# Latent attention on one NeuronCore: a third bank for the transposed scores, and the values products gathered into four runs a pair of heads

## What is computed

```
def _L1_attn_ref(x, latent_w, latent_b, Wd_w, Wd_b, out_w, out_b):
    ...
    Wdkv = x @ latent_w + latent_b
    q = jnp.einsum('btc,hcl->bhtl', x, Wd_w) + Wd_b[None, :, None, :]
    scores = jnp.einsum('bhtl,bsl->bhts', q, Wdkv) / jnp.asarray(np.sqrt(d_head), dtype=x.dtype)
    causal = jnp.tril(jnp.ones((t, t), dtype=bool))
    scores = jnp.where(causal[None, None, :, :], scores, -jnp.inf)
    attn = jax.nn.softmax(scores, axis=-1)
    y = jnp.einsum('bhts,bsl->bhtl', attn, Wdkv)
    z = jnp.transpose(y, (0, 2, 1, 3)).reshape(b, t, h * Wdkv.shape[-1])
    return z @ out_w + out_b
```

## Time and profile before

| | before |
|---|---|
| median of 3 runs | 3188.33 us |
| lowest and highest | 3187.82 and 3189.63 us |
| profiled execution | 3197.16 us |
| its span, first to last instruction | 3195.4 us |
| TensorE busy, mean granted clock | 2832.2 us (89%), 0.919 |
| VectorE busy | 2087.3 us (65%) |
| ScalarE busy | 1199.9 us (38%) |
| GpSimd busy | 836.7 us (26%) |

### The profile page before, as it was taken

One profiled execution on the slowest core, in us unless ns is written; L12 is line 12 of the kernel. 1 busy time (PEld: TensorE's weight loads), 2 busy tenths in 40 slices (PEclk: granted clock), 3 DMA queues, 4 the chain that ended last, 5 costly groups with the idle time before them and its releaser, 6 DMA issues. The chain is left out here.

```text
span 3195.4 us, 55424 instructions
## 1 busy us (share of the span) xinstructions
PE 2832.2 (89%) x15400; PEld 1924.1 (60%) x15400; DVE 2087.3 (65%) x5242; ACT 1199.9 (38%) x2164; POOL 836.7 (26%) x1220
## 2 busy tenths in 40 slices
PE   5999999958787888689999998869989989999986
PEld 4777777735555555467777776445465465465453
DVE  6777777747676777577777776355556556555533
ACT  2111111127565657521111111335545545545532
POOL 1222332225555555423222332001101101111100
PEclk8999999958888788899999998879999999999988
DMA  3000000000000000110000000000000000000000
GB/s 130 0 0 0 0 0 0 1 0 2 3 2 3 2 2 2 61 44 0 0 0 0 0 0 1 0 1 1 1 2 1 1 1 1 1 1 1 1 1 27
DMA packets 12996, 23.60 MB, mean 7 GB/s; under 512 B 2306, under 2 KB 7682, under 8 KB 12804
## 3 DMA queue, kind: packets, MB, share of 16 engines
q1 hardware_dynamic: 12804, 21.22, 2.0%
HBM read 18.52 MB, written 2.10 MB: 6 GB/s over the span
## 5 line engine op out<-in xcount | busy, mean ns | idle before, releaser
L555 DVE SCALAR_TENSOR_TENSOR moe_acc<-moe_ps,moe_comb,moe_acc 128x512 f32<-128x512 f32 x896 | 661.1, 744 | 174.5 <-PE moe_ps L304 167.9
L2017 DVE CUSTOM_DVE_ANT_0 attn_masked<-attn_psm,attn_causal 128x1024 f32<-128x1024 f32 (+7 forms) x512 | 367.6, 755 | 210.4 <-PE attn_psm L1742 199.3
L1921 ACT ACTIVATE attn_probs<-attn_pse 128x512 f32<-128x512 f32 (+1 forms) x640 | 319.9, 553 | 301.6 <-PE attn_pse L1756 301.0
L304 PE MATMUL moe_ps<-moe_Wg,moe_xh 128*128 128x512 f32 x1024 | 329.4, 403 | 25.0 <-DVE moe_Wu L501 25.0
L335 PE MATMUL moe_ps<-moe_Wd,moe_ih 128*128 128x512 f32 x1024 | 337.8, 411 | 0.0
L304 PE MATMUL moe_ps<-moe_Wu,moe_xh 128*128 128x512 f32 x1024 | 337.1, 411 | 0.0
L1772 PE MATMUL attn_psy<-attn_probs,attn_V 128*64 128x512 f32 (+3 forms) x1536 | 325.5, 524 | 0.3 <-POOL attn_probs L1677 0.3
L454 POOL TENSOR_SCALAR moe_part<-consts,moe_pick,moe_prob 128x8 f32<-128x8 f32 x256 | 98.1, 398 | 752.1 <-ACT moe_prob L389 752.1
L1677 POOL TENSOR_SCALAR_AFFINE_SELECT attn_probs<-attn_probs 128x256 f32<-128x256 f32 (+1 forms) x192 | 95.1, 495 | 757.7 <-ACT attn_probs L1921 757.7
L1021 POOL TENSOR_TENSOR attn_R<-attn_R 128x1024 f32<-128x1024 f32 (+1 forms) x128 | 215.5, 1690 | 201.6 <-DVE attn_R L1365 201.4
L1756 PE MATMUL attn_pse<-attn_qS,attn_kS 110*128 110x512 f32 (+3 forms) x768 | 233.2, 394 | 21.4 <-ACT attn_probs L1921 15.2
(11 more groups left out here) (208 smaller groups left out, 4871.2 us busy)
## 6 DMA issues: line engine op xcount, KB each, us to landing
moe_stageg<-in_w_gate SPq DMA_DIRECT2D x8, 512.0 KB, 7.2
moe_stageu<-in_w_up SPq DMA_DIRECT2D x8, 512.0 KB, 8.3
moe_stageg<-in_w_down SPq DMA_DIRECT2D x8, 512.0 KB, 3.7
out<-X SPq DMA_DIRECT2D x1, 2048.0 KB, 8.9
attn_qS<-attn_mh SPq DMA_DIRECT2D x64, 4.0 KB
attn_qS<-attn_ml SPq DMA_DIRECT2D x64, 4.0 KB
attn_wd<-in_wd SPq DMA_DIRECT2D x1, 864.0 KB, 5.7
attn_w<-in_wqkv SPq DMA_DIRECT2D x1, 768.0 KB, 5.1
```

What stands on the lines that cost most here:

```text
L304: last = pe.matmul(expert_bank[j % 4][:, :], a[q][:, :], w[b][:, cols], start=k == 0, stop=k == 2)
L555: dve.scalar_tensor_tensor(acc[:, q, r, :], expert_bank[j % 4][:, :], comb[:, q, r, e:e + 1], acc[:, q, r, :], ALU.mult, ALU.add).then_inc ...
L1921: act.activation(probs[:, u % 2, c, HALF - n:HALF], e_bank[c][:, HALF - n:HALF], ACT.Exp, scale=SCORE_SCALE).then_inc(p_ready, 1)
L2017: dve.tensor_tensor_reduce(masked[:, k % 2, 0:n], m_all[:, base:base + n], causal[:, SEQ - n:SEQ], 1.0, NEG, ALU.add, ALU.max, mx[:, q, v: ...
```

## The change

- `e_bank` has three banks, and the scores' tiles go round them: 18 tiles a pair, two for each wide unit and one for each narrow one, in whose single bank both heads lie side by side. A tile waits for the exponential of the tile three before it. ScalarE takes both heads of a narrow unit in one instruction of 128x2x256.
- `probs` has RING = 5 places for units instead of 2.
- The values stand in four runs: units 0 to 2 behind unit 3, units 3 to 5 behind unit 6, units 6 and 7 behind unit 8, units 8 and 9 in the next pair behind its first scores. `copy_out` of the second half goes there too.
- `o_bank` is gone. The maxima are transposed into bank 0 of `m_all`, the latent rows go to its bank 2, the output products to the third `e_bank`. The keys' and the transposed inputs' banks change places, and the projections go in the order of banks 2, 3, 0, 1. The first maxima of a pair wait for all four queries.
- The first two pairs of an element are written out, and the loop of pairs has two iterations.

```diff
+RING = 5
-        probs = sb("probs", [P, 2, 2, HALF])
+        probs = sb("probs", [P, RING, 2, HALF])
...
+        ORDER = (2, 3, 0, 1)
+        TOGETHER = ((0, 1, 2), (3, 4, 5), (6, 7), (8, 9))
+        NG = len(TOGETHER)
+        GROUP_OF = [g for g, us in enumerate(TOGETHER) for _ in us]
+        AFTER = {3: 0, 6: 1, 8: 2}
...
+        TILE = [0]
+        for u in range(NU):
+            TILE.append(TILE[-1] + (1 if narrow(u) else 2))
...
-                with eng.Fori(0, PAIRS // 2 - 1) as i:
+                for i in range(2):
+                    pair(b * PAIRS + i, i, i, b, (True, True))
+                with eng.Fori(1, PAIRS // 2 - 1) as i:
...
                 def scores(m, q, u):
                     s, pieces = units[u]
                     for c in range(2):
-                        pe.wait_ge(p_ready, after(m * 2 * NU + 2 * (u - 1) + c))
+                        n_, bank = TILE[u] + (0 if narrow(u) else c), e_bank[(TILE[u] + (0 if narrow(u) else c)) % 3]
+                        if c == 0 or not narrow(u):
+                            pe.wait_ge(p_ready, after(m * NT + n_ - 3))
...
                     for u in range(NU):
                         scores(m, q, u)
+                        if u == 0 and not first_pair:
+                            values(m - 1, NG - 1)
...
                         if u == NU - 1 and ahead[1] and not opens(i, ahead):
-                            project(m + 2, 1)
-                        if u >= 1:
-                            values(m, q, u - 1)
+                            project(m + 2, 0)
+                        if u in AFTER:
+                            values(m, AFTER[u])
...
                         if ahead[1] and not opens(i, ahead) and u == NU - 2:
-                            project(m + 2, 0)
+                            project(m + 2, 1)
                     if opens(i, ahead):
-                        for c in range(2):
+                        pe.wait_ge(v_ready, after(b + 1))
+                        for c in (1, 0):
                             project(m + 2, c)
-                    values(m, q, NU - 1)
+                    if last_pair:
+                        values(m, NG - 1)
```

More of the change, by code:

```diff
@@ L1757, in scores @@
                                              qS[q][c][:, s * HALF + qc:s * HALF + qc + n], start=True, stop=True)
-                        last.then_inc(s_ready, 1)
-                def values(m, q, u):
-                    s, pieces = units[u]
-                    first = u in (0, NQ0)
-                    if first:
-                        pe.wait_ge(yc_ready, after(m * 2 + s - 1))
-                    if u in DIAGONAL:
-                        pe.wait_ge(tri_ready, after(m * len(DIAGONAL) + DIAGONAL.index(u)))
-                    else:
-                        pe.wait_ge(p_ready, after(m * 2 * NU + 2 * u + 1))
-                    end = u in (NQ0 - 1, NU - 1)
-                    for k, (kt, at_, qc, n, _) in enumerate(pieces):
-                        for c in range(2):
-                            last = pe.matmul(y_bank[VW * c:VW * (c + 1), qc:qc + n], V[:, kt, :], probs[:, u % 2, c, at_:at_ + n],
-                                             start=first and k == 0, stop=end, skip_group_check=True)
-                    last.then_inc(y_ready if end else pv_ready, 1)
+                        if c == 1 or not narrow(u):
+                            last.then_inc(s_ready, 1)
@@ new lines, in values @@
+                def values(m, g):
+                    for u in TOGETHER[g]:
+                        s, pieces = units[u]
+                        first = u in (0, NQ0)
+                        if first:
+                            pe.wait_ge(yc_ready, after(m * 2 + s - 1))
+                        if u in DIAGONAL:
+                            pe.wait_ge(tri_ready, after(m * len(DIAGONAL) + DIAGONAL.index(u)))
+                        else:
+                            pe.wait_ge(p_ready, after(m * NT + TILE[u + 1] - 1))
+                        end = u in (NQ0 - 1, NU - 1)
+                        for k, (kt, at_, qc, n, _) in enumerate(pieces):
+                            for c in range(2):
+                                last = pe.matmul(y_bank[VW * c:VW * (c + 1), qc:qc + n], V[:, kt, :], probs[:, u % RING, c, at_:at_ + n],
+                                                 start=first and k == 0, stop=end, skip_group_check=True)
+                    last.then_inc(pv_ready, 1)
@@ L1779, in start @@
                     latent_rows(0)
-                    for c in range(2):
+                    pe.wait_ge(v_ready, after(0))
+                    for c in (1, 0):
                         project(0, c)
@@ L1783, in start @@
                         scores_max(0, 0, v, kN)
-                    pe.wait_ge(v_ready, after(0))
                     transpose_max(0, 0)
-                    for c in range(2):
+                    for c in (1, 0):
                         project(1, c)
@@ L1834, in output @@
                         pe.wait_ge(zc_ready, after((b * BT + j) * 2 + 1))
[L1835 to L1836 removed]
                         pe.wait_ge(res.xo_ready, after(b * BT + j - 1))
                         for k in range(5):
[L1839 removed]
+                            last = pe.matmul(e_bank[2][:, 0:P], zT[:, j % 2, k * P:(k + 1) * P], wo[:, k * P:(k + 1) * P], start=k == 0, stop=k == 4)
                         last.then_inc(o_ready, 1)
```

117 lines of the change are left out of this document (62 added, 55 removed).

## The result

| | before | after |
|---|---|---|
| median of 4 runs each | 3188.07 us | 3360.68 us |
| lowest and highest | 3187.57, 3189.63 | 3359.21, 3366.33 |
| ratio, 95% interval | | 1.0544 (1.0526 to 1.0562) |
| span of the profiled execution | 3195.4 us | 3358.8 us |
| TensorE busy, mean granted clock | 89%, 0.919 | 85%, 0.902 |

The change makes the kernel 172.6 us slower, where 121 were forecast. In the code after, maxima scores are L1759, transposed scores L1775, values L1793, projections L1745, the transposition of the maxima L1765, VectorE's maximum L2046.

A forecast was written before the change was run, and what follows sets the result against it. TensorE was taken to bound the latent attention phase, with the ring of maxima making it wait once values were gathered. Terms 110 - 2 - 11 + 2 + 22 gave +121 us, so 3309 us; range 3250 to 3375 us.

The forecast's parts named there:

- The walk: Latent attention pair, summed turn by turn: 27.78 us against 24.22, +3.56 a pair, +110 us over 31 pairs.
- The split of the 3.7 us a pair: Steady pair: TensorE works about 1.8 us less and waits some 5.4 us more, forecast as +3.56 a pair.
- switches: TensorE round trips into values and back: about 0.36 us each, 160 fewer, 58 us of its time.
- the clock: TensorE's granted clock falls through waiting: one fall in every second pair, 1.5 us each, +22 us (0 to +93).
- Rival 3: Attention pairs: the clock falls in nearly each stretch, slower by more, 3380 us; chance 0.15.
- the forecast with 0.60: Whole kernel: waits as walked and some falls of the clock, +121 us, 3309 us; chance 0.60.
- The table load: ScalarE's exponential table load before the loop of pairs: six of nine 1283 ns loads go, -11 us (5 to 14 saved).
- The projections' wait: Next element's projections wait until VectorE has taken the latent rows from their bank, three times: +2 us (0 to 3).
- the third bank: Score tiles: exponentials may lag three tiles, but the ring sets the turn whose 0.25 us wait goes: nothing.
- the DMA: Maxima's DMAs, 5.38 us from transposition to next scores: hidden in 5.5 us; if not, 0 to +10 us.
- last pair: The pair without maxima of a next pair gains five round trips: -2 us.
- the ring: Maxima n and n+2 share two banks, so TensorE waits for VectorE: turns of 2.20, 2.06 and 1.86 us.

The follow-up runs named there:

- e2_filled: Kernel after, with scores matmuls of units 1, 6 and 8 issued twice and of narrow units 2 and 5 four times; 3294.22 us, ratio 1.0333.
- e9_short_maxima: Kernel after, with VectorE reducing only 128 columns of each maximum and TensorE's work untouched; 3133.14 us in one run.
- e1: Kernel after, with values again in nine runs a pair, units 8 and 9 still in the next pair; 3218.02 us, ratio 1.0088.
- e3_table_out: Kernel before, with only the first two pairs of each element written out and two iterations in the loop; 3173.76 us, ratio 0.9951.

## Why the prediction was right, and where it was off

**Right: the sign, the mechanism, the length of a pair.** The walk gave 27.78 us; a pair without a fall lasts 27.93, and the waits stand where they were put (0.94, 1.02, 1.15, 0.78 and 0.96, where 1.0 or more was said, with one of 0.59 that was not). By the measured pair this term is 31 x (27.90 - 24.22) = 114 us, for 110; 27.90 is a steady pair of e2_filled. It is shown from four sides: filled gaps leave the length, a second place for the large maxima takes 2.1 us of it, six runs give what the walk gives, and a short VectorE part makes the same runs faster than before.

The split of the 3.7 us a pair was a little off: TensorE's work fell by 1.22 us (23.67 to 22.45), where 1.8 were forecast, and its idle time rose from 0.53 to 5.45, by 4.9 where 5.4 were. Five switches are thus worth 0.24 us each by busy time (0.30 with 22.18 us in e9_short_maxima), not 0.36, and the change saved 39 to 48 us of work, not 58. By the Trainium skill, page "TensorEngine Tiling (Array Packing)", section Key Properties, a change of the tiling mode drains TensorE. The trace agrees in so far as fewer changes came with less work; the drain itself is not seen.

**Off: the clock.** "One fall in every second pair at 1.5 us" gave +22; against e2_filled it was 66 us. Both factors were short. The clock was under 1.00 in 20 of 25 ordinary pairs, not in every second. And 1.5 us was the price of a fall on scores and short values runs of the kernel before; now a fall lands on a dense run, 4.54 for 2.37, and a pair grows by 2.4 to 3.1 us (30.3 to 31.0 for 27.9), two by 5.1 (33.0). Falls in the seventh and eighth pairs add 3.9 + 5.5 us by the table above. Rival 3 (3380) took two falls at 1.5 us in every pair and overshot: right in kind, 19 us too far. The measured time is 52 us above the forecast, so it lies nearer to this rival, which had a chance of 0.15, than to the forecast with 0.60; the range held it because it was drawn out towards the rival. The rule of the Trainium skill that stood beside it (page "TensorE: Matmul & The Clock Gate", section "A second HAM failure mode: psum-queue depth-cycling") is borne out here: with waits of 0.4 to 1.2 us on cycled banks the clock swung between 1.00 and 0.50, and with the gaps filled it stayed at 1.00 in the steady pairs. Its chance was set too low for want of such a stretch in the trace of before. The six runs, which keep four such waits and no fall, show that waits of this length don't always do it.

**The table load:** -11 forecast, -15.4 measured. Six loads went, three are left, as said, and the six pairs gave 10.9 us. By the profiles the rest lies in the seventh pairs (2.6 us less) and in the eighth and first ones together (3.8 less), and was not forecast. The longer wait at two element heads, also not forecast, is given back in the pairs behind it.

**The projections' wait:** +2 forecast, and the wait itself is 3 x 0.73 = 2.2 us. The whole rearrangement costs some 12, by the profiles 7.7 of it in the seventh pairs and 2.1 in the ordinary ones. The step had the wait right and left out the clock: two falls on the projections behind it cost 1.54 us each.

**Nothing for the third bank, nothing for the DMA:** both stand. The DMA was hidden, and e1 shows how narrowly: 0.82 us of wait as soon as the tail shrinks.

The sum as measured: 114 - 2 (last pair, not tested) - 15 + 12 + 66 = +175, beside 172.6. That it closes so well is in part luck. Between the profiles of e3_table_out and e2_filled the phase grows by 118 us (866.8 to 985.1). The 21 ordinary pairs that aren't the first of an element give 77.4 for 21 x 3.68 = 77.3, and the three seventh ones 17.2 for 11.0 + 7.7. But the four first pairs give only 6.5 for 14.7, and the three eighth pairs 17.3 for 11.0.

What stays open: why the unreleased wait at the element heads grows from 1.5 to 4.3 us when pairs are written out ahead of the loop; what decides whether a pair with waits falls; and why the eighth pairs grew by more than the ring. None was tried by itself.

## What to carry to other kernels

Before work of one kind is gathered into long runs, ask what each piece was covering where it stood: here the pieces filled the turns of a two-place buffer whose VectorE part didn't shrink, and saving 1.2 us of work in a pair brought 4.9 us of waits, 114 us net over the phase and 66 more by the clock. Give the buffer its second place first (3132.94 us with as many runs as before, of which some 15 us are the moved table load), and gather only where no wait needs the cover, as at the end of the pair (0.3 us a pair; 3130.22 us, the lowest median here, 1.8% under before). Price idle time on TensorE by the clock too, and by the densest work that stands behind it.

## What the hardware showed that was not expected

- Work added for its own sake made the kernel faster: 621 more matmul records in the phase (4647 for 4026 in the kernel after), and 66.5 us less. The waits shrank from about 1.0 to 0.3 to 0.6 us and the granted clock stayed at 1.00 in the steady pairs.
- Two pairs with the same first waits differ by the clock alone: 0.94 and 1.02 or 1.03 before the second and third maxima, then a values run of 2.37 in one and 4.54 in the other.
- A switch saved between maxima was worth nothing even where the ring had room (nine runs and six both give pairs of 23.0 to 23.3, with TensorE busy 22.8 to 22.9 us of them). Why the work didn't shrink is not shown. The only idle time left in the nine-run kernel's steady pairs stands before scores that wait for an exponential, in some of them, as in this row:

```profile
2458.11 0.99 PE L1777 MATMUL attn_pse<-attn_qS,attn_kS 110*128 110x384 f32 x4 [0.31 <-ACT attn_probs L1945]
```
